# Three loads of x, reordered heads and staged reads, and DVE casts for group 1 in a one-core audio tower kernel

## The reference

```python
interp = cubic_interpolate_1d(signal, 0.25)
windows = interp[:, idx]                       # [16, 249, 64]
kw = 0.5 * (windows + 1.3) ** 2 + 0.5 * jnp.exp(-0.5 * (windows - 0.7) ** 2)
M = jnp.abs(jnp.fft.fft(kw, axis=-1))
Mmax = jnp.max(M, axis=-1, keepdims=True)
Mt = M * jax.nn.sigmoid(M - 0.12 * Mmax)
h = soft_minimum(Mt, 0.9 * Mmax)               # -logsumexp(-a, -b)
n = layernorm(h)                               # eps = 1e-5
q, k, v = n @ Wq, n @ Wk, n @ Wv               # 8 heads of 64
attn = jax.nn.sigmoid(q @ k.T * 8)             # per head, over 249 tokens
h = h + jax.nn.relu((attn @ v) @ Wo)
n = layernorm(h)
h = h + shared_mlp(n) + top2_gated(experts_mlp(n), gates(n))
```

## Time and profile before

| | |
|---|---|
| median of 3 runs (range) | 169.74 us (169.63 to 171.81) |
| profiled execution | 169.56 us, of which span 167.7 us |
| PE busy | 150.6 us, 90% |
| ACT busy | 114.9 us, 69% |
| DVE busy | 107.4 us, 64% |
| POOL busy | 53.5 us, 32% |

### The profile page before, as it was taken

How to read it: one execution, slowest core, us unless ns; L and a number is a source line. 1 busy time by engine, 2 the same in 40 slices (tenths; PEclk the granted TensorE clock), 3 DMA queues, 4 the chain that set the end, 5 groups by cost and what they waited for, 6 DMA issues and landing times.

```text
span 167.7 us, 6718 instructions
## 1 busy us (share of the span) xinstructions
PE 150.6 (90%) x2856; PEld 90.8 (54%) x2856; DVE 107.4 (64%) x275; ACT 114.9 (69%) x157; POOL 53.5 (32%) x97
## 2 busy tenths in 40 slices
PE   7599493995996999999999999999999999999890
PEld 2259441443463657575756555544575565765580
DVE  1155898998675695867673848867359883443521
ACT  3388992996766897989987898737727637457420
POOL 3250006956651558182607153426200000000000
PEclk9879569999999999999999999999999999999999
DMA  5920000028567475948566700000000101001002
GB/s 129 199 103 4 0 0 0 0 89 216 132 185 228 122 223 148 262 115 203 138 179 179 189 18 4 0 4 4 0 21 16 34 5 31 24 11 30 21 16 57
DMA packets 14701, 14.00 MB, mean 83 GB/s; under 512 B 1288, under 2 KB 14444, under 8 KB 14608
## 3 DMA queue, kind: packets, MB, share of 16 engines
q1 hardware_dynamic: 14384, 13.42, 30.2%
q10 hardware_dynamic: 288, 0.16, 0.4%
HBM read 8.97 MB, written 4.60 MB: 81 GB/s over the span
## 4 chain that ended last, share of the span: by engine, by line
PE 65%; DVE 10%; DMA 9%; ACT 8%; issue 3%; SPq 2%; DVEq 0%
PE ps L420 12%; PE ps L440 12%; PE ps L541 8%; PE ps L559 7%; PE ps L598 6%; DMA YS<-y_stage 4%; PE ps L451 4%; ACT probs L1134 3%; DMA area<-x_in 3%; PE ps L568 3%; PE ps L297 3%; PE ps L583 2%; PE ps L312 2%; DMA y_stage<-YP 2%; SPq L262 2%
## 5 line engine op out<-in xcount | busy, mean ns | idle before, releaser
L1134 ACT ACTIVATE probs<-ps 125x1000 f32<-125x1000 f32 x64 | 61.8, 1009 | 11.0 <-PE ps L420 10.1
L440 PE MATMUL ps<-probs,xn 124*32 124x250 f32 (+1 forms) x512 | 39.3, 375 | 0.1
L420 PE MATMUL ps<-YS,XT 128*32 128x500 f16 x448 | 34.3, 376 | 3.5 <-DMA YS<-y_stage 3.4
L440 PEld LDWEIGHTS ps<-probs,xn 124*32 124x32 f32 (+1 forms) x512 | 15.9, 109 | 12.3 <-issue 2.5
L1166 ACT ACTIVATE H2r<-ps,wf 128x500 f32<-128x500 f32 x16 | 10.8, 677 | 15.4 <-PE ps L559 15.4
L802 DVE COPY ZS<-ps 128x250 f32<-128x250 f32 x32 | 12.9, 413 | 11.0 <-PE ps L440 10.9
L420 PEld LDWEIGHTS ps<-YS,XT 128*32 128x32 f16 x448 | 10.8, 96 | 11.8 <-DMA YS<-y_stage 4.3
L559 PE MATMUL ps<-area,wf 128*64 128x500 f32 x64 | 16.7, 585 | 0.0
L1004 DVE TENSOR_TENSOR area<-H2r,ps 128x500 f32<-128x500 f32 x16 | 10.8, 674 | 9.2 <-ACT H2r L1166 8.6
L1153 ACT ACTIVATE area<-ps,wf 128x500 f32<-128x500 f32 x24 | 15.9, 672 | 0.9 <-PE ps L541 0.9
L598 PE MATMUL ps<-wf,area 128*61 128x64 f32 (+1 forms) x384 | 14.0, 225 | 0.0
(11 more groups left out here) (151 smaller groups left out, 248.9 us busy)
## 6 DMA issues: line engine op xcount, KB each, us to landing
YS<-y_stage SPq DMA_DIRECT2D x56, 125.0 KB, 3.0
y_stage<-YP SPq DMA_DIRECT2D x14, 250.0 KB, 3.2
tower_out<-res SPq DMA_DIRECT2D x8, 124.0 KB
wf<-wf_in SPq DMA_DIRECT2D x1, 648.0 KB, 7.1
wa<-wa_in SPq DMA_DIRECT2D x1, 512.0 KB, 6.6
area<-x_in SPq DMA_DIRECT2D x1, 210.9 KB
ch<-ch_in SPq DMA_DIRECT2D x1, 160.0 KB, 6.1
tower_out<-res SPq DMA_DIRECT2D x8, 0.5 KB
```

The costliest lines, as they stand in the source:

```text
L420: last = mm(ps[k0:k1, 2 * (n % 2) + j, 0:TG].rearrange("p (h n) -> p h n", h=2), XT[:, g % 3, (2 * bb + cj) * P + k0:(2 * bb + cj) * P + k ...
L440: last = mm(ps[R * hh:R * hh + R, 4 + bb, half * TB:(half + 1) * TB], xn[0:keys, 4 * g + 2 * bb + cj, :], probs[0:keys, n % 3, hh, :], sta ...
L1134: fn(probs[:, n % 3].rearrange("p (j h) n -> p j (h n)", j=2), ps[0:P, 2 * (n % 2):2 * (n % 2) + 2, 0:TG], ACT.Sigmoid, scale=SCORE_SCALE) ...
```

## The change

- x comes in three loads (500, 500 and 1000 columns, `TAP_COLS`); the second waits only for DVE's zeroing of its columns, and the weights are issued only when the last part of x has landed.
- `distance` and its softplus are taken for rows 8 to 20 (`near`) first, and for rows 20 to 32 (`far`) behind the product of the weights.
- The layernorm of `first` folds eps into the sum, so `variance(first)` goes; the root of F is applied elsewhere. POOL squares `third`, and takes its groups 2 to 4 ahead of the splitting of the expert weights.
- Group 0: the parts 4 and 5 move behind `scores(0)` on PE, with both halves of `y_project(1, .)` in front of `scores(1)`; ACT takes their high halves behind `probs` of steps 1 and 2. DVE instead of ACT casts the projected queries of group 1.
- PE: `x_transpose` and `y_project` stand one step earlier (two in group 1: t = 1, 2, 3), `attn_out` one step earlier (one later in group 1), `x2_transpose` one step earlier.
- SP: from group 3 on the reads of k = 1 stand behind the first `send` of the next group.
- `layer3(6)` stands behind `layer2(7, 1)` instead of behind `layer2(7, 2)`.

```diff
@@ -41,7 +41,7 @@
 ALPHA, BETA = 0.12, 0.9
-PARTS = ((0, 0, 2), (1, 0, 3), (0, 1, 4), (1, 1, 5), (2, None, 6), (3, None, 5))
+PARTS = ((0, 0, 2), (1, 0, 3), (0, 1, 4), (1, 1, 5), (2, None, 4), (3, None, 5))
 EPS = 1e-5
@@ -64,6 +64,7 @@
 KV = 72
+TAP_COLS = (slice(0, 4 * P), slice(4 * P, 8 * P), slice(8 * P, NB * P))
@@ -231,11 +233,13 @@
         def _(sp):
-            for i, cols in enumerate((slice(0, 4 * P), slice(4 * P, NB * P))):
+            for i, cols in enumerate(TAP_COLS):
                 if i:
                     sp.wait_ge(pad_set, 1)
+                if i == 2:
                     sp.wait_ge(pad_pool, 1)
                 sp.dma_start(tapsT[0:TAPS, cols], x[:, cols]).then_inc(taps_in[i], 16)
+            sp.wait_ge(taps_in[2], 16)
             sp.dma_start(wa[:], wa_in).then_inc(attn_w_in, 16)
@@ -262,10 +266,14 @@
             for g in range(1, NG):
-                for k in range(2):
-                    send(g, k)
-                for k in range(2):
-                    read_back(g, k)
+                send(g, 0)
+                if g >= 4:
+                    read_back(g - 1, 1)
+                send(g, 1)
+                read_back(g, 0)
+                if g <= 2:
+                    read_back(g, 1)
+            read_back(NG - 1, 1)
             for g in range(NG):
@@ -372,7 +380,6 @@
                     pe.wait_ge(packed, 2)
-                    pe.wait_ge(yd_lo, 5)
                 else:
@@ -388,8 +395,8 @@
                     pe.wait_ge(wout_cp, 1)
-                if i == 5:
-                    pe.wait_ge(yd_lo, 4)
+                if i >= 4:
+                    pe.wait_ge(yd_lo, i - 1)
                 slot = 4 * (p % 2) + 2 * (p // 2)
@@ -497,29 +502,29 @@
                 if n == 0:
-                    y_part(5)
-                if n == 1:
-                    y_project(1, 0)
-                    y_project(1, 1)
+                    for i in (4, 5):
+                        y_part(i)
+                    for k in range(2):
+                        y_project(1, k)
                 if n == 6:
...
-                if t == (3 if g == 1 else 1) and 1 <= g < NG - 2:
+                if t == (1 if g == 1 else 0) and 1 <= g < NG - 2:
                     x_transpose(g + 2)
-                if t == (4 if g == 1 else 2) and 1 <= g < NG - 2:
+                if t == (2 if g == 1 else 1) and 1 <= g < NG - 2:
                     y_project(g + 2, 0)
-                if t == (5 if g == 1 else 4) and 1 <= g < NG - 2:
+                if t == 3 and 1 <= g < NG - 2:
                     y_project(g + 2, 1)
-                if t == (4 if g == 1 else 3) and g >= 1:
+                if t == (5 if g == 1 else 2) and g >= 1:
                     if g + 2 < NG:
...
                     attn_out(g - 1)
-                if t == 7 and g >= 2:
+                if t == 6 and g >= 2:
                     x2_transpose(g - 2)
@@ -624,6 +629,8 @@
                     layer2(g, 1)
+                if g == NG - 1:
+                    layer3(g - 1)
                 if g + 1 < NG:
@@ -640,7 +647,7 @@
                     layer1(g + 1, 3)
-                if 1 <= g <= NG:
+                if 1 <= g <= NG and g != NG - 1:
                     layer3(g - 1)
@@ -699,9 +706,12 @@
+            def masked_size(rows):
+                st.done(v.tensor_tensor(masked[:, rows, :], masked[:, rows, :], mag[:, rows, 0:NBIN], ALU.mult))
+
             def distance(rows):
-                st.wait(st.done(v.tensor_tensor(masked[:, rows, :], masked[:, rows, :], mag[:, rows, 0:NBIN], ALU.mult)))
+                st.wait()
                 dve1_at["dist", rows.start] = st.done(
@@ -720,9 +730,11 @@
             dve.wait_ge(act1, 3)
+            masked_size(first)
             distance(first)
             dve.wait_ge(act1, 4)
-            distance(others)
+            masked_size(others)
+            distance(near)
@@ -731,10 +743,14 @@
-            def total(rows, of):
+            def total(rows, of, plus=0.0):
                 st.wait()
-                st.done(v.tensor_tensor(norm[:, 1, rows], of[:, rows, 0], of[:, rows, R], ALU.add))
+                if plus:
+                    st.done(v.scalar_tensor_tensor(norm[:, 1, rows], of[:, rows, 0], -plus, of[:, rows, R],
+                                                   ALU.add, ALU.add))
+                else:
+                    st.done(v.tensor_tensor(norm[:, 1, rows], of[:, rows, 0], of[:, rows, R], ALU.add))
                 st.wait(st.done(v.tensor_reduce(norm[:, 0, rows], of[:, rows, 0:NBIN], AX_X, ALU.add)))
@@ -759,18 +775,18 @@
             square(first)
-            total(first, masked)
-            variance(first)
+            total(first, masked, F * EPS)
+            dve1_at["squares", first.start] = st.n
             dve.wait_ge(wprod_hi, 1)
...
                                    ALU.mult, ALU.subtract).then_inc(wprod_lo, 1)
-            dve.wait_ge(act1, 6)
-            soft_minimum(third)
+            distance(far)
...
             dve.wait_ge(rstd_done, 1)
-            st.wait(st.done(v.tensor_tensor(xn[:, rows, :], mag[:, rows, 0:R], wide(4, rows, R, norm), ALU.mult)))
+            st.wait(st.done(v.scalar_tensor_tensor(xn[:, rows, :], mag[:, rows, 0:R], float(F) ** 0.5, wide(4, rows, R, norm),
+                                                   ALU.mult, ALU.mult)))
             high, low, full = parts(rows)
@@ -919,21 +935,26 @@
+            dve.wait_ge(act1, 6)
+            soft_minimum(third)
             x_take(0)
             total(third, tok)
-            for i in range(4):
+            for i in range(2):
+                part_low(i)
+            centre(third)
+            for i in range(2, 4):
                 part_low(i)
             x_take(1)
-            part_low(4)
-            centre(third)
-            part_low(5)
-            square(third)
             y_take(1, 0)
+            dve.wait_ge(square_pool, 1)
             total(third, masked)
             variance(third)
+            part_low(4)
             y_take(1, 1)
+            part_low(5)
             z_take(0, 0)
+            dve.wait_ge(act1, 7)
             soft_minimum(later)
@@ -946,11 +967,11 @@
             y_take(2, 1)
+            x_take(3)
             z_take(1, 0)
-            x_take(3)
             y_take(3, 0)
+            y_take(3, 1)
             z_take(1, 1)
-            y_take(3, 1)
             z_take(1, 2)
@@ -980,8 +1001,8 @@
                     gate_scale(0)
+                x2_take(g - 2)
                 z_take(g, 2)
-                x2_take(g - 2)
                 squares2(g - 1)
@@ -1091,21 +1112,17 @@
             distance_plus(first)
-            distance_plus(others)
+            distance_plus(near)
             act.wait_ge(vfold_mm, 1)
...
                ACT.Copy, scale=QSCALE).then_inc(wprod_hi, 1)
+            distance_plus(far)
             act.wait_ge(idle_set, 1)
...
             fn(outW[:].rearrange("p a f -> p (a f)"), ps[:, 2, 0:2 * F], ACT.Copy).then_inc(wout_cp, 1)
-
-            def second_high(k):
-
-                act.wait_ge(y_mm, k + 1)
-                fn(YP[:, 1, 0, k, :], ps[:, y_bank(1, k), 0:TG], ACT.Copy).then_inc(y_hi, 1)
@@ -1133,10 +1150,8 @@
                    ACT.Sigmoid, scale=SCORE_SCALE).then_inc(s_act, 1)
-                if n == 0:
-                    part_high(5)
                 if n in (1, 2):
-                    second_high(n - 1)
+                    part_high(n + 3)
                 if n == 6:
@@ -1231,14 +1246,24 @@
-            inverse_deviation(slice(0, 4), first)
-            inverse_deviation(slice(4, 8), first)
+            pool.wait_ge(dve1, dve1_at["squares", first.start])
+            for g in range(2):
+                rows = slice(4 * g, 4 * g + 4)
+                v.tensor_tensor(norm[:, 4, rows], norm[:, 2, rows], half_neg[0:P, rows], ALU.pow).then_inc(rstd_done, 1)
+            pool.wait_ge(rstd_done, 2)
+            v.tensor_scalar(norm[:, 4, 4:8], norm[:, 4, 4:8], float(F) ** 0.5, None, ALU.mult).then_inc(rstd_done, 1)
             split_rows(1)
...
                               scoreW[:, :, 0, :].rearrange("p (i a j) r -> p i a j r", i=2, a=2)[:, :, k]).then_inc(packed, 1)
-
+            pool.wait_ge(dve1, dve1_at["centred", third.start])
+            v.tensor_tensor(masked[:, third, :], mag[:, third, 0:NBIN], mag[:, third, 0:NBIN],
+                            ALU.mult).then_inc(square_pool, 1)
+            inverse_deviation(slice(8, 12), third)
+            split_rows(2)
+            inverse_deviation(slice(12, 16), third)
+            split_rows(3)
             pool.wait_ge(ffn_w_in, 16)
@@ -1253,16 +1278,14 @@
             v.tensor_copy(wg[:, 1, :], w1l[:, G0:G0 + E]).then_inc(w1_split, 1)
-            inverse_deviation(slice(8, 12), third)
-            split_rows(2)
-            inverse_deviation(slice(12, 16), third)
-            split_rows(3)
-            inverse_deviation(later, later)
+            inverse_deviation(slice(16, 20), later)
+            split_rows(4)
```

(3 more changed lines are left out.)

27 lines of the change are left out of this document (13 added, 14 removed).

## The result

| | before | changed |
|---|---|---|
| median | 169.99 us (169.63 to 171.81, 4 runs) | 177.3 us (176.75 to 178.62, 4 runs) |
| profiled execution, its span | 169.56 us, 167.7 us | 176.75 us, 175.0 us |

The ratio is 1.042 (1.032 to 1.051): slower, and 0.5 us above the top of the predicted range. The span grew by 7.3 us where the sum said 4.3. I read it by milestones, since both kernels pass the same ones; the third column is the difference, the fourth what the sum had.

The account below looks back on a forecast made before the run. PE was taken as the bound of attention, with the serial front and group 1's staged reads outside it; -2.7 + 0.8 + 2.0 + 3.8 + 0.4 = +4.3 on 169.56 gave 173.9 us, range 168.8 to 176.8.

Parts of the forecast that it names:

- C: Group 1, steps 8 to 16: two new PE waits, ahead of x_transpose(3) and y_project(3, 1), net +2.0 us.
- D: Groups 2 to 5: PE waits about 1 us for XT ahead of y_project once a group, +3.8 us.
- E: The end: layer3(6) no longer covers the wait of layer3(7) for ACT, +0.4 us.
- A: The front: three loads of x let the last DFT end at 11.9 instead of 14.64 us, -2.7 us.
- B: Tokens and group 0: nothing gained or lost to the first part, then step 8 later, +0.8 us.
- the forecast's own sign of being wrong: In the changed profile: new waits below 0.5, clock below 1.00 after 24 us, or a group staying at 8.7.
- rival 4: Weights late: held back until x landed, wa takes 1.0 to 2.5 longer, folds wait; about 175.5 us, chance 0.10.
- Rival 1: Waits hidden: ACT is the real pace and its idle time swallows them; 169.5 us, chance 0.20.
- Rival 2: Faster: DVE runs ahead, z_take and x_take finish without PE waiting, only gains stay; 165.4 us, chance 0.10.
- At nothing: Items priced at zero: POOL's square of third, order of x2_take, z_take and attn_out, later k = 1 reads.
- Rival 3: Clock falls to half in the DFT or steps 9 to 12, 1.4 us each; 175.3, both 176.7; chance 0.18.

Follow-up runs that it names:

- run 4: Also called three_loads_only: kernel before with only x in three loads and the weights held back until the third has landed; 169.49 us, ratio 0.997.
- run 14: Changed kernel with x in the two loads of the kernel before and the weights not held back; 179.75 us, ratio 1.069.
- changed_again: The changed kernel itself, unchanged, measured again; 179.16 us, ratio 1.057.
- run 5: Changed kernel with TensorE's order of groups 1 to 5, VectorE's of group 1 and group 0's order taken back, split of distance kept; 171.05 us, ratio 1.016.
- undo_both: Changed kernel with TensorE's order of groups 1 to 5 and VectorE's order of group 1 taken back; 173.88 us, ratio 1.023.
- run 2: Changed kernel with group 1's order on TensorE and VectorE taken back, groups 2 on keeping the new order; 175.26 us, ratio 1.031.
- run 1: Also called undo_steady: changed kernel with TensorE's x_transpose, y_project and attn_out places taken back from group 2 on; 177.91 us, ratio 1.045.
- run 8: Changed kernel with seven dummy matmuls more, four ahead of x_transpose(0) and three behind it; 177.73 us, ratio 1.053.
- run 13: Also called steady_kept: changed kernel with all places of groups 2 to 7 taken back, groups 0 and 1 keeping the new order; 174.96 us, ratio 1.034.
- front_kept: Changed kernel with all orders and layer3(6) taken back; three loads, distance split, shorter variance and later second-half reads stay; 169.06 us, ratio 0.995.
- undo_x2: Changed kernel with TensorE's order of groups 1 to 5, VectorE's of group 1, and the places of x2_transpose and x2_take taken back; 170.89 us, ratio 1.013.

## Why the prediction was wrong, and where it was right

The direction and the mechanisms of C, D and E were right, the time was 3.4 us too low, and the step that failed is the price of PE's own work up to step 8, taken at full clock throughout: in A "So the limit becomes ACT, a square and an exponential per quarter" and "two quarters after 10.0 give 11.9", and the same in both terms of B. In the profile of the result these two quarters of the DFT, at half clock, ended at 12.99, and A, B and B gave +0.6 where the sum had -1.9: 2.5 of the 3.0 us by which it missed the span. The limit by ACT holds at full clock, where the eight matmuls of the interpolation take PE 3.99 us, 1.0 a quarter, less than ACT's 1.27. At the lower level, for all or most of them, they took 6.05 to 7.09, up to 1.8 a quarter, and PE sets the pace; and where the interpolation ran at full clock, the DFT, the folds or group 0 did not. The row was in my own hands: the earlier trace rows showed 0.51 in just this work. I named the fall as a rival at 0.18 and priced it once or twice at 1.4; it is the usual case, and the forecast's own sign of being wrong, a clock below 1.00 after 24 us, came true (27.9 to 31.4). Of the sixteen traces with three loads, three ended the last DFT at 11.9 to 12.3, near where I had put it, two at 13.0 (the first profile is one) and eleven at 13.5 to 14.4.

**A** (-2.7): -1.6 in the changed kernel's profile, -0.2 to -2.7 over the traces, -0.5 in the median of run 4, -0.6 by the medians or -2.0 by the ratios of run 14: smaller than forecast in most traces, and its size in the median not settled. The weights came in time: wa was issued at 5.05 and landed 4.9 us later, at 9.95, against 6.6 and my 11.9; rival 4 is out. By the Trainium skill, DMA: Bandwidth & Descriptors, section Anatomy of one DMA, cited in the prediction, the fixed cost of 2.0 us is one of DMAs that GpSimd issues; these go out from SP and ACT, so only the rows count for it.

**B** (0 to the first part): the gain of 0.5 by the shorter variance is there. From the DFT's end to the split of the weights changed_again took 10.91 us, three_loads_only 11.49. In the first profile the folds at 0.50 kept DVE waiting 0.54 and took it away (11.54). The wait for outW, 1.14, is the one I described, and it takes the gain back: from the DFT's end to the first part the traces with the split took 14.58 to 14.59, 14.53 before, so the term of 0 is right at full clock. So of the 1.8 by which the first part came later than 26.4, 1.1 is the DFT and 0.6 (15.22 against 14.59) the folds.

**B** (+0.8 behind it): +1.5 in the profile, +2.2 to +2.6 in the seven traces with two falls, +1.0 by the sum of rows for none (run 5). So the term is about right at full clock. In the first profile step 8 waited for YS, and the chain behind it can be read: the second half was complete at 36.25, 8.04 after the first part, where the sum had 36.9 - 29.15 = 7.75 (undo_both, without a fall ahead of `mix(0)`: sent at 35.84, 7.57 after); from its send to the fourth read 3.2 us passed and not 2.2, as the first read took SP 1.38 to issue; and the read landed in 3.16, where the sum took the middle of 3.0 to 4.5:

```profile
36.27 0.54 SPq L253
36.85 1.38 SPq L266
...
39.45 3.16 DMA YS<-y_stage
```

So 0.5 is the level of PE, 1.0 the issue of the reads, and landing and chain gave 0.8 back; why the issue was slow is not known. I had not seen the wait of 2 us ahead of `mix(0)`: by itself it is hidden behind the read, as I wrote of group 0's end. A fall behind it is not: in undo_both step 8 stands directly behind group 0, with no wait for YS.

**C** (+2.0, bounds 1.5 to 2.6): +2.2 in the first profile, 2.0 in the median of run 2. In four other traces with this order at full clock (runs 1, 8, 13, 14) the stretch took 13.7, +3.0, and `x_transpose(3)` waited 2.74 us where I had 2.1. The missing 0.7 looks like DVE's: total and variance of the later rows stood at 40.86 to 42.07 in three_loads_only, in the pause ahead of step 8; now that pause is short or gone and they stand between `z_take(0, 2)` and `z_take(0, 3)`, on the way to `y_take(2, 1)`. That it is this work rests on the traces alone; no run moved it.

**D** (+3.8): +4.0 in the profile, 4.2 in the median of run 13 (3.7 in its trace). Four waits of 0.86 to 0.88 us, groups of 9.64. Rival 1 is out: ACT's idle time hid nothing, it grew. Rival 2 too: the earlier trace rows already had DVE waiting for the mix.

**E** (+0.4): +0.5, layer3(7) waits 0.9 us for ACT. "At nothing" was wrong for one of its items: `x2_transpose` at head 6 costs 0.26 us a group as soon as `attn_out` stands at its old place. The reads of the second half behind the next send cost nothing: with them, front_kept's groups took 8.71 to 8.73.

**Rival 3** is what was right beside the forecast, at a place more than I had thought of, group 0. Its 176.7 is the value closest to the result. In the first profile it makes 1.1 in the DFT, 0.6 in the folds and 0.5 on the way to `mix(0)`, 2.2 of the 2.9 by which the sum missed the profiled execution; the other 0.7 are C, D and E, 0.1 to 0.2 each, and the reads of group 1. That the level makes the difference is shown where kernels with the same instructions in a stretch differ only in it (undo_both and undo_x2 from the first part to step 8: 14.45 and 15.43; steps 8 to 16 in changed_again and steady_kept: 15.99 and 13.68). What makes the clock fall in one execution and not in the next is not shown, and the dummies moved it without a gain in time.

## What to carry to other kernels

Where a profile shows TensorE changing its level in a stretch, cost every serial matmul there at both levels and ask again which engine sets the pace: a faster load ahead of it may only buy a wait for TensorE. Moving a consumer one step ahead on a bound engine costs the work that covered its producer's chain, once per pass of the loop; that could be read from two rows (1.07 a group at most, 0.92 measured). And a wait that goes may have been the time in which another engine caught up (here seen in traces only, C): look what it did in it.

## What was not expected of the hardware

- The granted clock's record reads 1.00 at the start in all traces; yet the 500-column fp32 matmuls took mostly 1037 to 1041 ns until 8 us or later in twelve of eighteen, and 582 ns from about 5 us on in five of the others; the kernel before ran them at 703 ns and, after its recorded fall at 7.0, at 1037. Durations tell the level there, the record does not.
- The level fell to 0.50 while PE was busy nearly all the time: in the changed kernel at 10.9, in the DFT of 64-column matmuls, PE having been busy 0.89 us or more in each microsecond since 4 us.
- The same program spreads by 1 to 7 us between executions (undo_steady 177.11 to 178.33, three_loads_only 167.91 to 174.46, the kernel before on three chips 167.31 to 174.49), as much as what most of these edits are worth.
